# First attention of a four-layer Flamingo-style block: layer norms, counts and positions on GpSimd, the queries' high part on ScalarE

## The chip, the cores and the metric

The kernel runs on one core of a Trainium2 chip. The metric is the device time of one execution in microseconds. The core has TensorE (PE), VectorE (DVE), ScalarE (ACT), GpSimd (POOL) and SyncE (SP, which here only starts transfers). Each engine works through its own list of instructions in order and waits on semaphores that others raise.

## What is computed

`x` is (4, 1024, 256), float32; the context has 4 x 154 rows.

```
x = x + tanh(g_xattn[0]) * attention0(layernorm(x), ctx)      # stablemax weights: s >= 0: s + 1, else 1 / (1 - s)
x = x + tanh(g_ffn[0])   * moe(layernorm(x))                  # 64 experts, top 8, at most 128 tokens each, plus a shared part
x = x + tanh(g_xattn[1]) * attention1(layernorm(x), ctx)      # softmax
x = x + tanh(g_ffn[1])   * butterfly_mlp(layernorm(x))
```

A token that goes to expert e gets the place "how many tokens before it chose e"; from place 128 on it is dropped. The places feed the lists of tokens by expert.

## The kernel before

The 4096 tokens lie in SBUF as 32 tiles of 128 x 256. They are worked on in 8 halves of 512 tokens (4 tiles). There are three stages with a barrier of all engines between them: the first attention with the routing (0 to 401 us), the experts with the shared part (401 to about 740 us), the second attention with the last layer. The change lies in the first stage.

A plan (`plan_first`) is a list of units such as `("norm", "q", h)` or `("count", h)`. Every engine runs through the same list and executes its own part of each unit, so that the order on all engines follows the list. Attention scores come in chunks: 20 a half, 160 in all. For each chunk PE makes the scores (L811, or L813 and L814), ACT squares and takes the reciprocal root (L1174, L1179), DVE makes the weight with a minimum and a maximum (`weight`, L1505), which also frees the bank of the scores, and PE multiplies with the values (L839, L834). The scores have five banks, so PE can't make chunk n before DVE has made weight n - 4 or so.

Between the chunks the plan puts the steps of the neighbouring halves, one step at a time:

- `query_steps`: statistics (`stats`, DVE, L1380 and L1389), reciprocal deviation (`rstd`, POOL, L1889 and L1894), the norm of four tiles into `normed` (`norm`, DVE, L1425), transposes (PE, L757), `q_feats` (ACT, L1143), the projection (PE, L800, two parts), `q_parts` (DVE: L1496 adds the bias and rounds to the high part, L1499 makes what is left), and transfers into the query stack (`send_q`, SP).
- `after_steps`: transposes back and division (L856, L1511, L1513), the output projection (L880, L885), `x_add` (DVE, L1526), statistics and norm into `rows` (same lines as above), transposes (L757), `send_rows`, gate logits (L900), `shift`, `top`, `pick` (DVE, L1535 to L1558: the mask of the eight chosen experts), `count` (PE: the counts of the tokens before, by products with masks and with the running sum `before`; DVE: four additions of a mask to that sum, L1582), `position` (DVE: L1591 to L1605) and, in halves 3 and 7, `gate_weights`.
- `keys_steps` for the next batch entry, beside halves 0, 2 and 4: `key_mask`, `key_rest`, `set_values` on DVE among others.

The statistics of a norm have two sets of buffers (`moments`, `rstd`), taken in turn. POOL has little else in this stage: it clears tiles at the start and makes `rstd` 16 times. After the last scores, one-hot tiles (`hots`, DVE, L1710 and L1713; ACT, L1273) are made from the positions and PE places them (L998), 18 of 32 tiles within the first stage.

```
            def weight(n):
                V.wait_ge(exped, n + 1)
                V.scalar_tensor_tensor(weights[n % 9][:, :], weights[n % 9][:, :], 1.0, score_bank[n % 5], ALU.min,
                                       ALU.max).then_inc(weighted, 1)
```

Of the kernel before, what the change touches and what calls it, by code (L numbers as in the profile page):

```python
# [18 lines left out]
P = 128  # L19
# [37 lines left out]
NB = 16  # L57
# [3 lines left out]
FAR = 4096.0  # L61
ZERO_ROWS = (TILES + 1) // 3
# [422 lines left out]
def build(nc, D, out):  # L485
    ctx = ExitStack()
    with ctx:
# [50 lines left out]
        with ExitStack() as scope:  # L538
# [48 lines left out]
            pos_i = s0("pos_i", [P, 2, HT, EXPERTS], I32)  # L587
# [57 lines left out]
        with ExitStack() as scope:  # L645
# [43 lines left out]
        pool_set, ln_var, ln_rstd, x_added, out_biased, hid_split = (  # L689
            sem(n) for n in ("pool_set", "ln_var", "ln_rstd", "x_added", "out_biased", "hid_split"))  # L690
# [3 lines left out]
        keys_split, queries_split, weighted, masked, rows_set, summed = (  # L694
            sem(n) for n in ("keys_split", "queries_split", "weighted", "masked", "rows_set", "summed"))
# [444 lines left out]
        def scalar_program(A):  # L1140
# [219 lines left out]
            units = {"key_round": key_round, "send_keys": send_keys, "lay_wk": lay_wk, "q_feats": q_feats_, "square": square,  # L1360
# [15 lines left out]
        def vector_program(V):  # L1376
# [27 lines left out]
            def norm(kind, h):  # L1404
                n = norm_no[kind, h]
                if kind == "q":
                    to = normed
                    if h:
                        V.wait_ge(*misc.filled(("turn_q", h - 1), CD - 1))
                elif kind == "r":  # L1410
                    to = rows
                    if h:
                        V.wait_ge(*misc.filled(("turn_rows", h - 1), CD - 1))
                        V.wait_ge(rows_out, 16 * h)
                else:
                    to = normed1
                    if kind == "f":
                        last_turn = ("turn_q1", h + 2) if h + 2 < HALVES else ("turn_f", h - 1)
                    else:
                        last_turn = ("turn_f", h - 3) if h >= 3 else ("turn_q1", h - 1)  # L1420
                    if (kind, h) != ("q1", 0):
                        V.wait_ge(*wide.filled(last_turn, CD - 1))
                V.wait_ge(ln_rstd, n + 1)
                for t in range(HT):
                    V.tensor_scalar(to[:, t, 0:DIM], x[:, HT * h + t, :], moments[n % 2][:, t, 0:1],  # L1425
# [65 lines left out]
            def q_parts(h, mo):  # L1491
                key = ("project_q", h, mo)
                if h and mo == 0:
                    wait_all(V, q_in[(h - 1) % 2], (h - 1) // 2 + 1)
                V.wait_ge(*misc.filled(key))
                V.tensor_scalar(q_stage[:, 0, mo, :], misc.ap(key), bq[:, mo:mo + 1], None,  # L1496
                                ALU.add).then_inc(queries_rounded, 1)
# [53 lines left out]
            def pick(h):  # L1551
# [5 lines left out]
                V.wait_ge(dve_own, own.n)  # L1557
                V.tensor_scalar(masks[:, :, :], picked[:, :, :], 0.0, None, ALU.is_gt).then_inc(masked, 1)  # L1558
# [15 lines left out]
            def count(h):  # L1574
                old, new = before[:, h % 2, :], before[:, (h + 1) % 2, :]
                V.wait_ge(masked, h + 1)
                for t in range(HT):
                    if t:
                        V.wait_ge(dve_own, own.n)
                    elif h:  # L1580
                        V.wait_ge(summed, h)
                    m = V.tensor_tensor(new, new if t else old, masks[:, t, :], ALU.add)  # L1582
                    if t < HT - 1:
# [740 lines left out]
```

## Time and profile before

| | us |
|---|---|
| Median of 3 runs | 1207.16 (1202.42 to 1209.33) |
| The profiled execution, its own time | 1211.06 |
| Its span, first to last instruction | 1209.2 |

| engine | busy us in the whole span | share |
|---|---|---|
| PE | 1030.5 | 85% |
| DVE | 790.1 | 65% |
| ACT | 624.0 | 52% |
| POOL | 384.1 | 32% |

Busy time is time with an instruction in execution; a group's row gives its sum, the mean of one in ns, and after the second bar the idle time of the engine just before it with what ended that. A timeline row has start, duration, engine, line and instruction, and in brackets the idle time before it. The chain of waits is the work that ended last, followed back from the end: where a piece stands on it, nothing shown would have let what follows start earlier.

### The profile page before, as it was taken

Reading aid. Unit: us, or ns where it says so; the run is one execution under the profiler, and the core shown is the slowest. Engines: PE = TensorE matmul, PEld = TensorE weight load, DVE = VectorE, ACT = ScalarE, POOL = GpSimd, SP = SyncE. Lnnn points to the kernel's source line nnn. Section 1 sums busy time; section 2 is a strip of 40 time slices with the busy share of each in tenths; the row PEclk is TensorE's granted clock in tenths of the full one; section 3 lists DMA queues with packets and bytes.
Section 4 is the critical chain, followed back from the end, with each engine's and each line's share of the span. In section 5 each row is a group of like instructions: output and inputs, shape, how many; then the busy total and the mean of one; then the engine's idle time right before and its main releaser. Section 6 shows DMA issues by size and latency. Waiting matters only on the chain.

```text
span 1209.2 us, 17329 instructions
## 1 busy us (share of the span) xinstructions
PE 1030.5 (85%) x5635; PEld 750.4 (62%) x5635; DVE 790.1 (65%) x1991; ACT 624.0 (52%) x1185; POOL 384.1 (32%) x385
## 2 busy tenths in 40 slices
PE   3998898698876679989898967889888988999987
PEld 2445455354444567878687757567676766767666
DVE  5677877866777756664667566766757575664433
ACT  2786656757846425564554431455545554544532
POOL 6000000000000023776767622233434243514234
PEclk9798979979997889999999995899999999999989
DMA  6564542632121434888878653421322232120001
GB/s 156 147 160 131 156 133 69 184 108 53 49 105 53 143 116 91 187 215 232 200 190 181 127 140 72 113 83 29 104 54 75 68 88 71 51 56 1 20 1 35
DMA packets 101561, 128.41 MB, mean 106 GB/s; under 512 B 31136, under 2 KB 73504, under 8 KB 101216
## 3 DMA queue, kind: packets, MB, share of 16 engines
q1 hardware_dynamic: 87088, 106.32, 30.8%
q0 software_dynamic: 12288, 18.88, 8.7%
q10 hardware_dynamic: 2096, 2.10, 0.8%
q8 instruction: 46, 0.75, 0.3%
q14 instruction: 43, 0.35, 0.1%
HBM read 66.15 MB, written 30.70 MB: 80 GB/s over the span
## 4 chain that ended last, share of the span: by engine, by line
PE 55%; DVE 25%; ACT 6%; issue 5%; POOL 3%; DMA 2%; ACTq 1%; SPq 0%; DVEq 0%; POOLq 0%
PE psum L1118 6%; PE psum L932 6%; PE psum L1103 5%; PE psum L839 4%; PE psum L1021 4%; PE psum L811 4%; PE psum L948 4%; DVE stats L1380 3%; PE psum L885 3%; DVE weights L1505 2%; DVE peaks L1790 2%; PE psum L834 2%; PE psum L800 2%; PE psum L1050 2%; PE psum L757 2%
## 5 line engine op out<-in xcount | busy, mean ns | idle before, releaser
L1889 POOL TENSOR_SCALAR vareps<-moments 128x4 f32<-128x4 f32 x32 | 10.4, 324 | 483.8 <-DVE moments L1389 483.8
L811 PE MATMUL psum<-q_stack,k_stack 97*128 97x512 f32 (+1 forms) x256 | 124.1, 513 | 38.6 <-DVE weights L1505 21.4
L1316 ACT ACTIVATE weights<-psum 128x512 f32<-128x512 f32 x160 | 93.8, 595 | 69.5 <-PE psum L811 59.5
L1909 POOL DMA_INDIRECT expert_sums<-made,sum_rows x64 | 104.9, 1639 | 62.5 <-DVE made L1754 43.0
L1505 DVE SCALAR_TENSOR_TENSOR weights<-weights,psum 128x512 f32<-128x512 f32 x160 | 101.8, 679 | 22.5 <-ACT weights L1179 22.3
L1790 DVE TENSOR_REDUCE peaks<-psum 128x2 f32<-128x308 f32 x256 | 107.0, 470 | 12.3 <-PE psum L1052 12.0
L1050 PE MATMUL psum<-k_stack,q_stack 96*128 96x256 f32 x256 | 86.4, 391 | 28.6 <-DVE peaks L1790 16.7
L932 PE MATMUL psum<-feat_parts,w_shared_up 128*128 128x512 f32 x384 | 98.3, 406 | 6.4 <-DVE shared_silu L1628 2.8
L1174 ACT ACTIVATE weights<-psum 128x512 f32<-128x512 f32 x160 | 88.8, 594 | 28.9 <-PE psum L811 28.5
L1118 PE MATMUL psum<-w_con_high,hidden 128*128 128x256 f32 x512 | 103.3, 300 | 0.5 <-POOL hidden L1941 0.5
L1941 POOL TENSOR_TENSOR hidden<-hidden_whole,hidden 128x512 fp32r<-128x512 f32 x64 | 82.4, 1293 | 63.8 <-DVE hidden L1838 63.8
L1901 POOL DMA_INDIRECT got<-rows_scratch,tokens x64 | 68.4, 1069 | 99.8 <-DVE sum_rows L1741 80.6
L811 PEld LDWEIGHTS psum<-q_stack,k_stack 97*128 97x128 f32 (+1 forms) x256 | 50.0, 200 | 79.3 <-issue 44.6
L1838 DVE CAST hidden<-hidden_whole 128x512 fp32r<-128x512 f32 x64 | 44.8, 704 | 81.2 <-ACT hidden_whole L1345 80.6
L1179 ACT ACTIVATE weights<-weights 128x512 f32<-128x512 f32 x160 | 94.0, 634 | 1.0
L1103 PE MATMUL psum<-feats,w_up_high 128*128 128x512 f32 x256 | 79.7, 408 | 14.2 <-ACT hidden_whole L1345 8.9
L1118 PEld LDWEIGHTS psum<-w_con_high,hidden 128*128 128x128 f32 x512 | 81.6, 192 | 14.0 <-POOL hidden L1941 6.9
L1050 PEld LDWEIGHTS psum<-k_stack,q_stack 96*128 96x128 f32 x256 | 52.9, 207 | 53.4 <-DVE peaks L1790 21.9
L932 PEld LDWEIGHTS psum<-feat_parts,w_shared_up 128*128 128x128 f32 x384 | 71.7, 193 | 22.0 <-DVE shared_silu L1628 3.6
L1021 PEld LDWEIGHTS psum<-got_t,expert_w 128*128 128x128 f32 x512 | 65.8, 195 | 24.9 <-ACT got_t L1280 15.9
L1021 PE MATMUL psum<-got_t,expert_w 128*128 128x128 f32 x512 | 72.1, 285 | 10.5 <-DVE inner L1747 5.5
L839 PE MATMUL psum<-weights,values 128*32 128x512 f32 x512 | 78.0, 675 | 0.7 <-ACT turned L1186 0.7
(212 smaller groups left out, 2315.7 us busy)
## 6 DMA issues: line engine op xcount, KB each, us to landing
expert_w<-in_expert_w SPq DMA_DIRECT2D x64, 384.0 KB
q_stack<-q_stage SPq DMA_DIRECT2D x96, 128.0 KB, 2.5
q_stack<-q_stage SPq DMA_DIRECT2D x174, 64.0 KB, 2.0
expert_sums<-zeros SPq DMA_DIRECT2D x6, 1408.0 KB, 8.1
fetched<-expert_sums SPq DMA_DIRECT2D x14, 512.0 KB, 4.9
k_raw<-in_k SPq DMA_DIRECT2D x16, 300.0 KB
x<-in_x SPq DMA_DIRECT2D x8, 512.0 KB, 4.5
rows_scratch<-rows SPq DMA_DIRECT2D x8, 512.0 KB, 2.9
```

What stands on the lines that cost most here:

```text
L811: T.matmul(to, k[0:row, head_at(head), :], q[0:row, head // 2, :], start=True, stop=True).then_inc(scored, 1)
L839: m = T.matmul(to[32 * j:32 * j + 32, :], vals[:, 0, 4 * g + j, :], w[(n + j) % len(w)][:, :], start=True, stop=False, tile_position=(0, 3 ...
L932: m = T.matmul(shared_banks(h).ap(key, half), w_sgu[:, pw, a:a + P], sh_parts[:, pf, c * HALF:(c + 1) * HALF], start=n == 0 and c == 0, st ...
L1021: m = T.matmul(bank[2][:, part * P:(part + 1) * P], expert_w[e % 8][:, c, part * INNER:(part + 1) * INNER], got_t[e % 3][:, c, :], start=c ...
L1050: T.matmul(view[:, :, 0:P], q[0:STACK, p, t * P:(t + 1) * P], keys[0:STACK, 2 * p:2 * p + 2, :], start=True, stop=True)
L1103: m = T.matmul(wide.ap(key), up_parts[pw][:, c, k * P:(k + 1) * P], feats[:, pf, c, :], start=i == 0 and c == 0, stop=i == 2 and c == CD - 1)
L1118: m = T.matmul(out_bank[t // 2][:, t % 2 * DIM:(t % 2 + 1) * DIM], hidden[k][:, ph, t * P:(t + 1) * P], con_parts[pw][:, BURST * b + k, :] ...
L1179: A.activation(weights[n % 9][:, :], weights[n % 9][:, :], ACT.Abs_reciprocal_sqrt).then_inc(exped, 1)
L1316: A.activation(weights1[n % 6][:, :], score_bank[n % 2], ACT.Exp).then_inc(exped, 1)
L1505: V.scalar_tensor_tensor(weights[n % 9][:, :], weights[n % 9][:, :], 1.0, score_bank[n % 5], ALU.min, ALU.max).then_inc(weighted, 1)
L1790: V.tensor_reduce(peaks[h % 2][:, t, 2 * p:2 * p + 2], view, AX.X, ALU.max).then_inc(wide.frees(key, i), 1)
L1909: G.indirect_dma_start(sum_dram[e % SUMS], bass.IndirectOffsetOnAxis(ap=sum_rows[:, e:e + 1], axis=0), made[e % 4][:, :], None, bounds_che ...
```

## The change

The layer norms of kind "q" (queries) and "r" (rows) are written by POOL, right behind its `rstd`, and no longer by DVE; DVE keeps the norms of the second attention and the last layer. The high part of the queries is made by ACT (Identity with the bias) instead of DVE. The running sum of masks (`count`) is made by POOL and left out for the last half, where nobody reads it. Of `position` DVE keeps the instruction that reads PSUM; six instructions on POOL, in float32 instead of integers, follow. Waits are added where an engine now reads what another writes: DVE's aggregate of moments waits for the norm that read that buffer (two norms back), `pick` for `summed`, `position` and `hots` for `positioned`.

```
-                V.tensor_scalar(q_stage[:, 0, mo, :], misc.ap(key), bq[:, mo:mo + 1], None,
-                                ALU.add).then_inc(queries_rounded, 1)
+            def q_parts(h, mo):                                    # ScalarE
+                key = ("project_q", h, mo)
+                if mo == 0:
+                    if h:
+                        wait_all(A, q_in[(h - 1) % 2], (h - 1) // 2 + 1)
+                    else:
+                        A.wait_ge(wq_in, 32)
+                A.wait_ge(*misc.filled(key))
+                A.activation(q_stage[:, 0, mo, :], misc.ap(key), ACT.Identity,
+                             bias=bq[:, mo:mo + 1]).then_inc(queries_rounded, 1)
...
+                if kind in ("q", "r") and n >= 2:                  # VectorE, statistics
+                    V.wait_ge(ln_normed, HT * (n - 1))
...
-            def count(h):                                          # VectorE
-                old, new = before[:, h % 2, :], before[:, (h + 1) % 2, :]
...
-                V.scalar_tensor_tensor(picked[:, :, :], masks[:, :, :], -FAR, counts, ALU.mult,
+                if h:
+                    V.wait_ge(positioned, h)
+                V.scalar_tensor_tensor(ranks[:, 0, :, :], masks[:, :, :], -FAR, counts, ALU.mult,
                                        ALU.add).then_inc(misc.frees(key), 1)
-                V.wait_ge(*misc.freed(key))
-                V.tensor_scalar(picked[:, :, :], picked[:, :, :], FAR, None, ALU.add)...
-                V.tensor_copy(pos_i[:, 0, :, :], picked[:, :, :])...
-                V.tensor_scalar(pos_i[:, 1, :, :], pos_i[:, 0, :, :], 4, None, ALU.logical_shift_right)...
-                V.tensor_scalar(pos_i[:, 0, :, :], pos_i[:, 0, :, :], NB - 1, None, ALU.bitwise_and)...
-                V.tensor_copy(pos_a[:, HT * h:HT * h + HT, :], pos_i[:, 1, :, :])
-                V.tensor_copy(pos_b[:, HT * h:HT * h + HT, :], pos_i[:, 0, :, :])
...
+            def norm_first(n, h, to, turned_before):               # GpSimd, called at the end of rstd
+                if h:
+                    G.wait_ge(*misc.filled(turned_before, CD - 1))
+                G.wait_ge(ln_rstd, n + 1)
+                for t in range(HT):
+                    G.tensor_scalar(to[:, t, :], x[:, HT * h + t, :], moments[n % 2][:, t, 0:1],
+                                    rstd[n % 2][:, t:t + 1], ALU.subtract, ALU.mult).then_inc(ln_normed, 1)
...
+            def count(h):                                          # GpSimd
+                if h == HALVES - 1:
+                    return
+                ...                                                # waits for masks, for PE's last count, four additions
+            def position(h):                                       # GpSimd, each waits for the one before
+                G.wait_ge(*misc.freed(("count", h)))
+                block, first = rank_block[:, :, :], ranks[:, 0, :, :]
+                G.tensor_scalar(block, first, BLOCK_MIDDLE, 1.0 / NB, ALU.subtract, ALU.mult)...
+                G.tensor_scalar(block, block, WHOLE, 0.0, ALU.add, ALU.add)...
+                G.tensor_scalar(block, block, -WHOLE, 0.0, ALU.add, ALU.add)...
+                G.tensor_scalar(pos_a[:, HT * h:HT * h + HT, :], block, FAR / NB, 0.0, ALU.add, ALU.add)
+                G.tensor_scalar(ranks[:, 1, :, :], block, float(-NB), 0.0, ALU.mult, ALU.add)...
+                G.tensor_tensor(pos_b[:, HT * h:HT * h + HT, :], ranks[:, 1, :, :], first, ALU.add).then_inc(positioned, 1)
```

## Rows read from the trace of the kernel before

**Rows 1.** Windows of the span: busy us (count) by engine, clock, DMA share, GB/s.
```profile
30.00:346.00 316.00, 275.01 (x1239) 151.89 (x1239) 236.21 (x651) 211.72 (x399) 16.43 (x26) 0.90 0.43 118
346.00:401.00 55.00, 30.93 (x180) 23.25 (x180) 41.27 (x105) 28.37 (x40) 1.56 (x2) 0.84 0.20 71
```

**Rows 2.** Waits of PE from 60 to 340 us: total, times, longest.
```profile
PE psum L811 <- DVE weights L1505: 19.9, 16, 3.4
PE psum L757 <- DVE rows L1425: 5.0, 7, 1.4
PE psum L757 <- DVE probs L1540: 3.5, 3, 1.5
```

**Rows 3.** Timeline of PE around the count and position of half 2.
```profile
191.91 1.00 PE L811 MATMUL psum<-q_stack,k_stack 97*128 97x512 f32 x2 [1.26 <-DVE weights L1505]
...
195.28 1.22 PE L811 MATMUL psum<-q_stack,k_stack 97*128 97x512 f32 x2 [1.49 <-DVE weights L1505]
```

**Rows 4.** Chain of waits, 186 to 196 us: start, us, piece.
```profile
190.31 0.19 DVE mask_sums L1582
...
191.17 1.20 DVE weights L1505 x2
192.36 0.34 DVE picked L1591
...
192.73 0.30 DVE picked L1594
...
194.53 0.61 DVE weights L1505
```

**Rows 5.** Chain of waits, 208 to 224 us, beside the keys' steps.
```profile
213.07 1.29 DVE rows L1425 x4
...
217.62 1.04 POOL rstd L1894
...
218.76 1.39 DVE normed L1425 x4
...
222.61 0.40 DVE probs L1540
```

**Rows 6.** Groups of DVE to 480 us: busy us, mean ns, idle before.
```profile
L1496 DVE TENSOR_SCALAR q_stage<-psum,bq 128x512 fp32r<-128x512 f32 x16 | 12.0, 748 | 18.3 <-PE psum L800 18.2
L1425 DVE TENSOR_SCALAR normed<-x,moments,rstd 128x256 f32<-128x256 f32 x32 | 11.0, 409 | 6.7 <-POOL rstd L1894 6.7
```

**Rows 7.** Groups of POOL, in both parts of the span (split at 480 us).
```profile
L1894 POOL TENSOR_TENSOR rstd<-vareps,minus_half 128x4 f32<-128x4 f32 x16 | 16.7, 1044 | 2.2
...
L1959 POOL MEMSET zeros<- 128x256 f32 x1 | 0.3, 316 | 0.1
...
L1928 POOL TENSOR_TENSOR x<-x,fetched 128x256 f32<-128x256 f32 x56 | 40.1, 746 | 49.2 <-DMA fetched<-expert_sums 39.6 <-DVE k_stack L1774 8.5 <-POOL x L1928 0.2
...
L1941 POOL TENSOR_TENSOR hidden<-hidden_whole,hidden 128x512 fp32r<-128x512 f32 x64 | 82.4, 1293 | 63.8 <-DVE hidden L1838 63.8
```

**Rows 8.** Groups of ACT to 480 us.
```profile
L1143 ACT ACTIVATE q_feats<-psum 128x512 f32<-128x512 f32 x16 | 9.2, 597 | 27.6 <-PE psum L757 27.6
...
L1228 ACT ACT_TABLE_LOAD x2 | 2.6, 1283 | 0.0
```

**Rows 9.** Timeline, the end of the stage: the last rows' norm.
```profile
362.65 1.25 POOL L1894 TENSOR_TENSOR rstd<-vareps,minus_half 128x4 f32<-128x4 f32 x1
...
369.69 1.38 DVE L1425 TENSOR_SCALAR rows<-x,moments,rstd 128x256 f32<-128x256 f32 x4
370.25 2.00 PE L757 MATMUL psum<-ident,rows 128*128 128x128 f32 x7 [8.86 <-DVE rows L1425]
```

**Rows 10.** Chain of waits, the last transfer before the barrier.
```profile
397.07 3.82 DMA rows_scratch<-probs
```

**Rows 11.** Timeline of the start.
```profile
8.14 1.38 DVE L1425 TENSOR_SCALAR normed<-x,moments,rstd 128x256 f32<-128x256 f32 x4 [1.57 <-POOL rstd L1894]
...
18.81 0.84 ACT L1156 ACTIVATE k_stage<-k_masked 128x768 fp32r<-128x768 f32 x1 [6.47 <-DVE k_masked L1465]
```

More of the change, by code:

```diff
@@ L61 @@
 FAR = 4096.0
+BLOCK_MIDDLE, WHOLE = (NB - 1) / 2, 1.5 * 2 ** 23
 ZERO_ROWS = (TILES + 1) // 3
@@ L1572, in gate_weights @@
                                        ALU.mult, ALU.mult).then_inc(rows_set, 1)
-            def count(h):
-                old, new = before[:, h % 2, :], before[:, (h + 1) % 2, :]
[L1576 to L1583, printed above, removed]
-                        m.then_inc(dve_own, own.up())
-                m.then_inc(summed, 1)
             def position(h):
@@ L1709, in hots @@
                     V.wait_ge(placed, i - HOTS + 1)
+                V.wait_ge(positioned, i // HT + 1)
                 V.tensor_tensor(hot_a[i % HOTS][:, :, :, :], a_iota[:, :, :, :],
@@ L1873, in gpsimd_program @@
         def gpsimd_program(G):
-            set_ = Own()
+            set_, own = Own(), Own()
             def clear_values(vals):
@@ L1894, in norm_rstd @@
                 G.tensor_tensor(rstd[n % 2][:, :], vareps[n % 2][:, :], half_pow[:, :], ALU.pow).then_inc(ln_rstd, 1)
+                if kind == "q":
+                    norm_first(n, h, normed, ("turn_q", h - 1))
+                elif kind == "r":
+                    if h:
+                        G.wait_ge(rows_out, 16 * h)
+                    norm_first(n, h, rows, ("turn_rows", h - 1))
+            def norm_first(n, h, to, turned_before):
+                if h:
+                    G.wait_ge(*misc.filled(turned_before, CD - 1))
[3 more added lines that the diff above has]
+                                    rstd[n % 2][:, t:t + 1], ALU.subtract, ALU.mult).then_inc(ln_normed, 1)
             def gather(e):
@@ L1942, in hidden_rest @@
                                 ALU.subtract).then_inc(hid_split, 1)
+            def count(h):
+                if h == HALVES - 1:
+                    return
+                old, new = before[:, h % 2, :], before[:, (h + 1) % 2, :]
+                G.wait_ge(masked, h + 1)
+                if h:
+                    G.wait_ge(*misc.filled(("count", h - 1)))
+                if h:
+                    G.wait_ge(summed, h)
+                for t in range(HT):
+                    if t:
+                        G.wait_ge(pool_own, own.n)
+                    m = G.tensor_tensor(new, new if t else old, masks[:, t, :], ALU.add)
+                    if t < HT - 1:
+                        m.then_inc(pool_own, own.up())
+                m.then_inc(summed, 1)
+            def position(h):
+                G.wait_ge(*misc.freed(("count", h)))
+                block, first = rank_block[:, :, :], ranks[:, 0, :, :]
+                G.tensor_scalar(block, first, BLOCK_MIDDLE, 1.0 / NB, ALU.subtract, ALU.mult).then_inc(pool_own, own.up())
+                G.wait_ge(pool_own, own.n)
+                G.tensor_scalar(block, block, WHOLE, 0.0, ALU.add, ALU.add).then_inc(pool_own, own.up())
+                G.wait_ge(pool_own, own.n)
+                G.tensor_scalar(block, block, -WHOLE, 0.0, ALU.add, ALU.add).then_inc(pool_own, own.up())
+                G.wait_ge(pool_own, own.n)
+                G.tensor_scalar(pos_a[:, HT * h:HT * h + HT, :], block, FAR / NB, 0.0, ALU.add, ALU.add)
+                G.tensor_scalar(ranks[:, 1, :, :], block, float(-NB), 0.0, ALU.mult, ALU.add).then_inc(pool_own, own.up())
+                G.wait_ge(pool_own, own.n)
+                G.tensor_tensor(pos_b[:, HT * h:HT * h + HT, :], ranks[:, 1, :, :], first, ALU.add).then_inc(positioned, 1)
             def set_query_ones(i):
@@ L1972, in gpsimd_program @@
             G.wait_ge(pool_set, set_.n)
-            units = {"rstd": norm_rstd, "load_rest": clear_rest, "gather": gather, "down": scatter,
+            units = {"rstd": norm_rstd, "count": count, "position": position, "load_rest": clear_rest, "gather": gather, "down": scatter,
                      "add_experts": add_experts, "bias_out": bias_out, "up": hidden_rest, "clear_v1": clear_v1}
```

53 lines of the change are left out of this document (16 added, 37 removed).

## The prediction

> **What bounds the kernel now.** I read the busy shares by window first, then PE's waits, then the chain of waits and the timeline at the places that they point to. From 30 to 346 us PE is busy 275 of 316 us, DVE 236, ACT 212 and POOL only 16 [rows 1]. PE is the bound, but 41 us of this stretch it stands still. The waits say for what: half of its idle time from 60 to 340 us is the wait for a weight of DVE [rows 2], and the timeline shows two pauses of one size, 1.26 and 1.49 us, at every half [rows 3]; I found the pair at halves 0, 1, 2, 3 and 4 (in half 3 the second is 3.4 us, the longest of rows 2, since `gate_weights` joins it) and the same chain of DVE pieces at half 5. The chain shows what DVE did instead of weights: the four additions of `count` before the first pause, the seven instructions of `position` before the second [rows 4]. So the stage isn't bound by DVE's sum, it is bound by DVE's bursts. From 346 to 401 us DVE is the bound itself, busy 41 of 55 us [rows 1], and what ends the stage is the transfer of `probs`, which starts when DVE is through with position and gate weights [rows 10]. Nothing behind the barrier is touched.
>
> **What leaves DVE.** 64 norm tiles at 0.41 us (the row has half of them), 16 high parts at 0.75 [rows 6], 32 additions at 0.19, and six instructions of `position` eight times, 0.30 each [rows 4]. That is 26 + 12 + 6 + 14 = 58 us, some 54 if the overlap of neighbours is taken out (four norm tiles take 1.38 us together [rows 9]). This isn't the gain: only what PE or the stage's end waited for counts. Step by step:
>
> **Count and position, halves 0 to 5.** Without `count` (190.31 to 191.17) the two weights start 0.86 us earlier, and a little more since DVE no longer makes the high part: ACT does it in about 0.60 in place of 0.76. I take 1.0 of the 1.26. Of `position` DVE keeps the 0.34 us piece; the 1.8 us from 192.73 to 194.53 go [rows 4]. The root that the next weight needs is done long before, so the second pause closes in full: 1.5. 6 x 2.5 = **-15.0 us**. POOL's part of position is six dependent instructions. By the bounds below some 0.6 us each, 3.6 us; only `hots` of half 7's tiles, which come behind the barrier, could meet it late, and POOL is idle there. I cost it at nothing; should it be 3 us late it would still end before the transfer of rows 10 lands. POOL's load in a half is then about 2.7 (rstd and variance, twice) + 4.4 (eight norm tiles) + 1.4 (count) + 3.6, 12 of 43 us: not a bound.
>
> **The price of a norm tile on POOL.** No row shows this instruction there. The lower bound is a clear of the same 128x256 tile, 0.32 us, which reads nothing; the upper one is an addition of two such tiles, 0.75 [rows 7]. It reads one tile, so it lies between; I take the middle, 0.55. Four tiles: 2.2 us against 1.38 on DVE.
>
> **Norm of the rows (8 times).** It lies on PE's path: `x_add`, statistics, rstd, norm, transposes. The tiles come one by one and PE transposes behind them; before, the first is ready 0.42 us after the start, now 0.55, and the last 2.2 instead of 1.38. In the four halves without keys' steps (1, 3, 5 and 6) the transposes end about 0.8 us later, but DVE, which normed there after a wait for rstd, has its next weights 1.4 us earlier and more. I take a net **+0.5 each, +2.0 us**. In halves 0, 2 and 4 DVE is the chain [rows 5]: rows 1.29, later a wait for POOL's rstd (1.04) and normed 1.39, then the keys' rest, weights and probs, for which PE waits 3.5 us in three times [rows 2]. These three pieces go off DVE, 3.7 us; POOL's rows end at about the same time as DVE's did, since they start at once and not behind the keys' masks. PE's pauses there are up to 1.4 us for rows and 1.5 for probs [rows 2]. Of these 2.9 I take **-2.0 each, -6.0 us**: behind DVE, PE's own gate products come due next. The norm of the queries is covered by the chunks' work between it and its transposes: PE's waits of rows 2 are for rows and never for normed. If that cover were gone it would cost 0.8 us a half, as with rows.
>
> **The queries' high part.** 16 activations of 128x512 from PSUM, 0.60 each [rows 8], in place of 0.75 on DVE. DVE waited 18.3 us in all for the projection before them [rows 6]; ACT, which is in order too, now waits there, and squares and roots queue behind it. DVE still waits, for ACT. ACT is idle around the second part in every half (its busy sum is 212 of 316 us), so I cost it at **0**; bounds: +9.6 us if every activation delays a root that is due, -2.4 if the shorter time shows every time.
>
> **The end of the stage.** The last norm of rows was ready for DVE at 363.9 but began at 369.69, behind DVE's splitting of the shared weights; PE waited 8.9 us for it [rows 9]. POOL does it at once. But the next consumer, ACT's row features, stands behind one-hot tiles that DVE makes, and DVE works on without a break: so only DVE's own 1.38 us come off, **-1.4**. Half 6: count and position, 2.8 us of DVE, lie between the last weight and the divisions for which PE and ACT wait: **-2.8**. Half 7: the same, right ahead of the gate weights and the last transfer [rows 10]: **-2.8**. Sum **-7.0 us**.
>
> **The start.** Before the first scores everything is one chain. The first norm on POOL ends 0.8 us later than DVE's 1.38 [rows 11], the high parts save 0.15 to 0.3, and ACT's second high part now comes before its rounding of the keys (0.84), which eats that. **+0.6 us.** POOL's clearing starts 0.8 later; DVE's first values wait for it, but its first weights wait for ACT's root behind that, which covers it.
>
> **Sum.** -15.0 + 2.0 - 6.0 + 0 - 7.0 + 0.6 = -25.4 us. The profiled execution took 1211.06 us, so its like would take 1185.7. It stands 3.9 us above the median of the runs, 1207.16; from the median I get 1181.8, and forecast **1182**.
>
> **A rule against it.** The rstd that ran while DVE compared one-hot tiles took 1.25 us [rows 9], the mean is 1.04 [rows 7]; most of the others ran beside nothing but weights. So POOL is slowed by some DVE work. The Trainium skill, "SBUF — State Buffer", on the shared port pair, says why: a DVE instruction with two SBUF inputs and a GpSimd instruction that reads SBUF exclude each other for its whole length; the trace agrees with a delay of that kind. DVE's weights read one input from PSUM and are no such instruction by that rule; the one-hot comparisons are.
>
> **Rivals.**
> (a) *DVE and POOL exclude each other at the end of the stage.* There DVE makes one-hot tiles all the time, and POOL gets 2.2 us of norm and twice 3.6 of position, plus a count of 1.4: 10.8 us. If DVE stood still for as long as POOL runs, the 7.0 gained are gone and 3.8 more: 1182 + 10.8 = 1193. For: the 1.25 us. Against: what was slowed there is POOL, and only by 0.2.
> (b) *ACT takes the place of DVE.* Each half's two high parts (9.6 us in all) delay roots, and ACT takes over DVE's wait for the projection, up to 12.4 of the 18.3 us in the steady stretch. All of it would leave -25.4 + 22 = -3.4: 1204. For: the roots follow the squares at once in ACT's list. Against: ACT's idle time.
> (c) *Slower: the norm on POOL is dear.* Rows' norms are on the path eight times with four tiles each, so each 0.1 us on a tile is 3.2 us. The gain is gone at 0.55 + 25.4 / 32 = 1.34 us a tile; at 1.5 the time is 1212. Nearest row for: 128x512 with two inputs takes 1.29 [rows 7], and a mere 4 elements with `pow` 1.04. Against: that is twice the tile and twice the inputs.
> (d) *Slower: ACT reloads its table.* If Identity isn't in the set that holds the root, each high part brings two loads of 1.28 us [rows 8]: 16 x 2.56 = 41 us on ACT, time 1223. Against: ACT's copies of this stage need none.
> (e) *More is gained.* PE's clock is 0.90 on average there [rows 1] because it falls to 1.2 GHz for stretches; with fewer pauses it may fall less. With all pauses of rows 2 closed and some of that, -40: 1167.
>
> **How the numbers follow.** The forecast's case gets 0.66, its own range 1171 to 1195 (half to all of the pauses, a tile from 0.32 to 0.75, which alone is -7 to +6 us); (a) 0.12, (b) 0.08, (c) 0.04, (d) 0.02, (e) 0.08. A measurement of this kernel can tell about 0.5% (6 us) from no change. Faster by more than that: 0.66 + 0.12 + 0.08 = 0.86; within: (b), 0.08; slower: 0.06. The range that leaves out 2 in 10 is 1168 to 1198: it holds (a), and leaves out most of (e), (b), (c) and (d).
>
> **What the profile would show.** Right: the pauses of PE before L811 in each half fall from 1.26 and 1.49 to under 0.3 and 0; norm tiles on POOL take 0.4 to 0.75 us; rows' transposes begin as soon as their norm does, and no pause there is over 1.5; the barrier falls near 376 us in place of 401; DVE's busy time falls by some 54 us, ACT's rises by 9.6; the other stages keep their lengths within 2 us. Wrong: tiles above 1 us on POOL, table loads between chunks, PE waiting for ACT's roots after the projection (b), one-hot comparisons longer than before (a), or the same pauses with a new releaser.

## The result and the profile after

| | before | after |
|---|---|---|
| Median | 1206.72 (1202.12 to 1211.06, 11 runs) | 1220.64 (1213.09 to 1223.28, 11 runs) |
| Ratio after / before | | 1.0115, 95% interval 1.0094 to 1.0136 |
| Profiled execution, its span | 1211.06, 1209.2 | 1222.56, 1220.8 |
| Barrier behind the first attention (PE's first product of the next stage) | 401.04 | 413.02 |
| From the barrier to the end | 808.2 | 807.8 |
| Busy: PE, DVE, ACT, POOL | 1030.5, 790.1, 624.0, 384.1 | 1036.8, 741.9, 633.0, 519.7 |

The kernel became slower by 1.15% (some 14 us), where 25 us were to be gained. The loss lies in the first stage alone: its barrier comes 12.0 us later, and what follows takes as long as before (807.8 against 808.2). DVE did lose its work (-48 us busy) and ACT took the 9 us that were forecast. Both profiled executions are slower than their medians, by 4.3 and 1.9 us. So the question is what in the first stage ate 37 us, from the forecast barrier at 376 to the measured 413.

Here are the busy shares of the kernel after by window, for the same two stretches as [rows 1] (busy us and count of PE, PE's weight loads, DVE, ACT, POOL; granted clock; DMA share; GB/s):

```profile
30.00:346.00 316.00, 268.32 (x1194) 148.07 (x1194) 188.44 (x496) 218.77 (x412) 126.97 (x144) 0.87 0.44 120
346.00:401.00 55.00, 36.04 (x188) 24.49 (x188) 36.68 (x97) 25.64 (x38) 17.83 (x16) 0.80 0.19 67
```

In the same 316 us PE issued 45 matmuls fewer than in [rows 1], at a granted clock of 0.87 in place of 0.90. POOL went from 16 to 127 us, and DVE is idle for 128 us. PE's waits from 60 to 340 us, which answer to [rows 2] (total, times, longest):

```profile
PE psum L760 <- POOL rows L1888: 24.2, 26, 1.4
PE psum L814 <- DVE weights L1507: 7.4, 11, 1.8
PE psum L760 <- POOL normed L1888: 3.4, 4, 0.9
```

The waits for DVE's weights fell from 19.9 to 7.4 us, as the steps on count and position wanted. But the wait of the transposes for rows rose from 5.0 us in 7 times to 24.2 in 26: PE now waits for each tile by itself. The groups of POOL show why (busy us, mean ns; these answer to [rows 7]):

```profile
L1888 POOL TENSOR_SCALAR rows<-x,moments,rstd 128x256 f32<-128x256 f32 x32 | 42.9, 1352 | 1.6 <-POOL rstd L1875 1.5
L1888 POOL TENSOR_SCALAR normed<-x,moments,rstd 128x256 f32<-128x256 f32 x32 | 38.7, 1221 | 1.3 <-POOL rstd L1875 1.2
L1959 POOL TENSOR_SCALAR rank_block<-ranks 128x256 f32<-128x256 f32 x8 | 8.7, 1089 | 48.1 <-DVE ranks L1584 48.0
...
L1966 POOL TENSOR_SCALAR ranks<-rank_block 128x256 f32<-128x256 f32 x8 | 3.5, 444 | 0.5
```

A norm tile takes 1.22 us on POOL, not 0.55, and lies outside the bound of 0.75 that an addition of two such tiles gave. (The 1.35 in the rows' line is a mean that the last four tiles raise; see the end of the stage.) The prediction had named tiles above 1 us as a sign that it was wrong. L1959 (subtract, multiply) and L1966 (multiply, add) read and write tiles of the same form, 128x256 of f32, with constants as factors, and differ in the pair of operations: 1.09 against 0.44 us. The high part on ACT took 0.69 us a piece (0.60 forecast), with no table load beside it:

```profile
L1192 ACT ACTIVATE q_stage<-psum,bq 128x512 fp32r<-128x512 f32 x16 | 11.0, 686 | 19.5 <-PE psum L803 19.5
```

A second thing shows when the stage is cut at the statistics of the rows of halves 5, 6 and 7. Two windows, first of the kernel before, then of the kernel after, with the same 145 and 139 matmuls in them:

```profile
298.92:329.75 30.83, 27.33 (x145) 15.22 (x144) 24.35 (x70) 25.04 (x48) 1.26 (x2) 1.00 0.14 48
329.75:362.19 32.44, 24.45 (x139) 14.22 (x138) 25.92 (x78) 15.65 (x27) 1.26 (x2) 1.00 0.26 98
```

```profile
297.68:335.03 37.35, 32.29 (x145) 18.30 (x144) 20.92 (x56) 25.11 (x48) 12.76 (x17) 0.82 0.12 40
335.03:374.56 39.53, 28.99 (x139) 16.66 (x138) 23.35 (x64) 15.76 (x27) 13.34 (x17) 0.83 0.22 80
```

Up to here the kernel after was 1.2 us ahead (297.68 against 298.92). It loses 13.6 us in these two. Of this 9.5 us is PE's busy time (27.33 to 32.29, 24.45 to 28.99) for the same products: the granted clock fell from 1.00 to 0.82. The timeline of PE shows the place:

```profile
298.22 1.09 PE L814 MATMUL psum<-q_stack,k_stack 97*128 97x512 f32 x2
300.68 0.30 PE L760 MATMUL psum<-ident,rows 128*128 128x128 f32 x1 [1.37 <-POOL rows L1888]
301.79 0.33 PE L760 MATMUL psum<-ident,rows 128*128 128x128 f32 x1 [0.82 <-POOL rows L1888]
302.99 0.33 PE L760 MATMUL psum<-ident,rows 128*128 128x128 f32 x1 [0.87 <-POOL rows L1888]
304.19 1.33 PE L760 MATMUL psum<-ident,rows 128*128 128x128 f32 x5 [0.87 <-POOL rows L1888]
...
309.19 3.51 PE L903 MATMUL psum<-gate_w,row_feats 128*128 128x65 f32 x16
```

```profile
298.00:304.00 6.00, 2.02 (x6) 0.79 (x5) 2.57 (x5) 2.69 (x5) 5.73 (x5) 0.98 0.02 4
304.00:306.00 2.00, 1.81 (x7) 1.46 (x7) 0.00 (x0) 1.04 (x2) 0.14 (x1) 0.50 0.47 157
306.00:316.00 10.00, 10.00 (x33) 6.04 (x32) 4.51 (x18) 4.62 (x10) 0.00 (x0) 0.50 0.33 113
```

PE is busy for 2.0 of 6 us in the waits for four tiles; behind them the clock stands at 0.50 (1.2 GHz) for 12 us, and the gate logits take 3.51 us, 1.90 in undisturbed halves. The waits cost a second time here, after they are over.

The end of the stage, the last rows' norm (answers to [rows 9]):

```profile
376.48 9.03 POOL L1888 TENSOR_SCALAR rows<-x,moments,rstd 128x256 f32<-128x256 f32 x4 [0.21 <-POOL rstd L1875]
377.51 2.36 DVE L1592 TENSOR_TENSOR w_shared_up<-shared_staging,w_shared_up 128x1024 fp32r<-128x1024 f32 x2 [1.19 <-ACT w_shared_up L1226]
377.85 0.45 PE L760 MATMUL psum<-ident,rows 128*128 128x128 f32 x1 [4.09 <-POOL rows L1888]
379.79 1.22 DVE L1597 TENSOR_TENSOR feat_parts<-feats_m,feat_parts 128x1024 fp32r<-128x1024 f32 x1
380.92 1.42 DVE L1601 TENSOR_TENSOR w_shared_down<-shared_staging,w_shared_down 128x1024 fp32r<-128x1024 f32 x1
381.99 0.48 PE L760 MATMUL psum<-ident,rows 128*128 128x128 f32 x1 [3.69 <-POOL rows L1888]
```

Four tiles take 4.84 us elsewhere and 9.03 here. PE had the first tile at 377.85, the second at 381.99, the third at 384.26. So the second took some 4.2 us: it lay beside DVE's four splits with two SBUF inputs (377.51 to 382.34) and was ready only 0.35 us before the last of them ended. The third took 2.3 us, beside DVE's one-hot comparisons. DVE hardly suffered (one split 1.42, the others of their kind 1.22). At the start (answers to [rows 11]) nothing covers the first norm; the first scores come at 30.89, where they came at 27.16 before:

```profile
8.33 4.84 POOL L1888 TENSOR_SCALAR normed<-x,moments,rstd 128x256 f32<-128x256 f32 x4
...
30.89 1.19 PE L814 MATMUL psum<-q_stack,k_stack 97*128 97x512 f32 x2 [5.97 <-DMA k_stack<-k_stage]
```

### The profile page after: what moved, and what is told of

Its sections match the earlier page's. It is cut to its first block, busy times and chain, and to the rows that moved or that the text cites. A ratio compares the mean times of both kernels' runs of the same rounds, so it can differ in the third digit from the quotient of the medians.

```text
span 1220.8 us, 17380 instructions
## 1 busy us (share of the span) xinstructions
PE 1036.8 (85%) x5635; PEld 755.4 (62%) x5635; DVE 741.9 (61%) x1831; ACT 633.0 (52%) x1201; POOL 519.7 (43%) x525
## 4 chain that ended last, share of the span: by engine, by line
PE 55%; DVE 17%; POOL 10%; ACT 8%; issue 6%; DMA 2%; SPq 1%; ACTq 1%; DVEq 0%; POOLq 0%
PE psum L935 5%; PE psum L1121 5%; PE psum L842 4%; PE psum L1106 4%; PE psum L1024 4%; PE psum L814 4%; PE psum L951 4%; POOL rows L1888 3%; PE psum L888 3%; PE psum L837 3%; PE psum L760 2%; PE psum L1053 2%; DVE stats L1394 2%; DVE peaks L1771 2%; PE psum L803 2%
## 5 line engine op out<-in xcount | busy, mean ns | idle before, releaser
L1177 ACT ACTIVATE weights<-psum 128x512 f32<-128x512 f32 x160 | 88.2, 594 | 20.6 <-PE psum L814 20.6
```

## The experiments

A ratio stands against runs of the kernel before on the same chip in the same job, with its 95% interval; 0.001 of it is 1.2 us. "Barrier" is PE's first product of the next stage in the profiled execution (before 401.04, after 413.02). That is one execution of each kernel, and two pairs of them show how far it can be trusted: with the high part alone changed the barrier came 5.2 us sooner (395.82) at a ratio of 1.0012, and with quicker positions in the multiply-add kernel it came 6.0 us later (389.25 against 383.22) at an unchanged ratio. Differences of some 6 us between barriers tell nothing by themselves; the length of a piece of the stage that an edit touches is steadier.

**Which part costs, which gains.** Both norms (queries and rows) back on DVE, all the rest of the change kept:

```
+on_vector = lambda kind, h: kind in ("q", "r")
...
-                if kind in ("q", "r"):                             # VectorE's norm
+                if kind in ("q", "r") and not on_vector(kind, h):
                     return
```

> The changed kernel with both first-stage norms back on VectorE; count, position and the queries' high part stay moved. Theory A (the price of a norm tile on GpSimd, 1.22 us where I took 0.55, is the whole of the loss; the rest gains what I forecast): about -20 us against the kernel before, so 1185 to 1190, the pauses before the scores gone, the first scores at 27 us again. Rival B (the moved count, position or high part cost something as well, for instance by ScalarE's roots coming later): 1200 or more.

Measured 1183.88 us, ratio 0.9769 (0.9715 to 0.9823), barrier 375.65; it is a little below the expected 1185 to 1190. Counts, positions and high part together gain 28 us, and the norms on POOL lose 42 on top of them (0.0346). The complement, norms alone on POOL (counts, positions and high part back on DVE):

> The kernel before with only the norms of queries and rows on GpSimd. Theory A: the loss of the changed kernel (+14) and the gain of the other parts (-20) come apart: 1235 to 1245, with both pauses per half (1.26 and 1.49 us) still there. Rival B: near the changed kernel, 1215 to 1222.

Measured 1240.94, ratio 1.0253 (1.0199 to 1.0307), barrier 434.28: slower by 31 us. PE waits 22.4 us for rows there from 60 to 340 us, and the 18.2 us for weights are back. The same norms cost 31 us here and 42 where the other parts had moved: the two losses seem to hide a part of each other. The difference of 11 us (0.0093) is only just clear of the noise of these runs (0.008).

The first of these divided again. The high part alone on ACT (`q_parts` as in the change, everything else as before):

> The kernel before with one part of the change: ScalarE makes the queries' high part; norms, counts and positions stay on VectorE. The prediction costed this at 0 (bounds +9.6 and -2.4), and gave count and position all of the -25 us that remain with the norms on VectorE. If that is right: 1206 to 1211 us and the same pauses before PE's chunk scores as in the kernel before. Rival: ScalarE's high parts lengthen the chain of roots (rival b): 1212 to 1218. Other rival: the high part brings a gain of its own, since VectorE's weights no longer queue behind its 0.75 us, twice a half: 1195 to 1204.

Measured 1207.78, ratio 1.0012 (0.9992 to 1.0031): no difference. PE's pauses for weights stay:

```profile
PE psum L814 <- DVE weights L1517: 20.2, 17, 2.6
```

Counts and positions alone on POOL:

> The kernel before with another part alone: counts and positions on GpSimd, high part and norms on VectorE. By the prediction's terms (-15.0 in halves 0 to 5, -5.6 at the end of the stage) about 1188 us, 1184 to 1192, and the pair of pauses of PE at count and position (1.26 and 1.49 us) gone but for some tenths. Rival: the high part is worth half of the gain of 25 us that both have together, then 1195 to 1200.

Measured 1187.00, ratio 0.9829 (0.9791 to 0.9866), barrier 377.94, and the pauses are down to

```profile
PE psum L815 <- DVE weights L1523: 5.6, 10, 0.8
```

That is -20.6 us by the ratio; the forecast's two terms were -15.0 and -5.6. The high part on top of it may give some us (0.9769 against 0.9829, intervals that overlap; barrier 2.3 us earlier); this isn't settled.

**Which of the norms.** The whole change, with rows on DVE and queries on POOL:

> The changed kernel with the norm of the rows back on VectorE, that of the queries still on GpSimd. Theory A: what is left of the loss is the start (first scores at 31 us, +3.7) and nothing in the loop, since the queries' norm is covered: 1188 to 1196. Rival (the queries' norm costs as much as the rows'): 1204 or more.

Measured 1208.85, ratio 0.9989 (0.9951 to 1.0028), barrier 396.75: in the range of the rival, not of the theory. The queries' norm is not covered. With it alone on POOL the transposes wait for single tiles:

```profile
PE psum L761 <- POOL normed L1901: 10.8, 13, 0.9
```

The projection behind them runs at a lower clock (granted 0.57 from 183.5 to 187.0 us):

```profile
180.77 0.33 PE L761 MATMUL psum<-ident,normed 128*128 128x128 f32 x1 [0.88 <-POOL normed L1901]
181.97 0.77 PE L761 MATMUL psum<-ident,normed 128*128 128x128 f32 x5 [0.88 <-POOL normed L1901]
...
183.54 3.38 PE L804 MATMUL psum<-q_feats,wq 128*128 128x512 f32 x4 [0.33 <-ACT q_feats L1147]
```

With both norms on DVE the same projection ran at a granted clock of 1.00 (169.5 to 172.0 us):

```profile
169.51 1.98 PE L804 MATMUL psum<-q_feats,wq 128*128 128x512 f32 x4 [0.22 <-ACT q_feats L1147]
```

The fourth corner, queries on DVE and rows on POOL:

> The whole change, but the queries' norm stays on VectorE and the rows' norm is on GpSimd with tiles of 1.2 us. The fourth corner of a square: both norms on VectorE 1183.9, both on GpSimd 1220.6, queries' alone on GpSimd 1208.9. If the two norms cost independently, 1220.6 - 25 = 1196 us (1192 to 1200), with no pause of PE at the start of the span and rows waits of some 24 us in the steady stretch. If they share one queue and block each other, the rows' norm alone costs more than 12 us and the time is 1200 to 1210.

Measured 1214.54, ratio 1.0067 (1.0030 to 1.0104), barrier 405.53: outside both ranges. Against both on DVE, rows alone cost 36 us (0.0298), queries alone 27 (0.0220), both 42 (0.0346). Each alone costs much, and they overlap, although each has its own tiles and its own time on POOL. A plain delay on the path would add up.

**Does the clock add to what the waits cost?** The whole change, and PE fills the waits between tiles with work that has no use:

```
                         m = T.transpose(ring.ap(key, c)[:, t * P:(t + 1) * P], src[:, t, c * P:(c + 1) * P],
                                         ident[:, :])
+                        if c == 0 and t < HT - 1 and kind[0] in ("q", "r"):
+                            for _ in range(4):
+                                T.transpose(ring.ap(key, c)[:, t * P:(t + 1) * P], src[:, t, c * P:(c + 1) * P],
+                                            ident[:, :])
```

> The whole change, and PE repeats the transpose of a tile four times (some 0.2 us each) while it waits for the next tile of a norm that GpSimd makes; data, order and all other engines are untouched, and PE only gets more work. Theory: the waits of 0.9 us for single tiles cost twice, once as idle time and once because the granted clock falls to 1.2 GHz behind them (in halves 6 and 7 PE's same work took 32.3 and 29.0 us in place of 27.3 and 24.5). Then the clock stays up: 1205 to 1213 us, granted clock of the first 401 us at 0.90 or more. Rival: only the waiting itself costs, and the clock falls for another reason; then the time is 1220 or some us more.

Measured 1207.82, ratio 0.9988 (0.9960 to 1.0017), barrier 399.78. PE got 192 matmuls more and the kernel became some 13 to 15 us faster than the whole change. In half 6, behind the rows' transposes, and then the window of 316 us:

```profile
296.60 1.08 PE L818 MATMUL psum<-q_stack,k_stack 97*128 97x512 f32 x2
...
299.17 1.90 PE L907 MATMUL psum<-gate_w,row_feats 128*128 128x65 f32 x16
```

```profile
30.00:346.00 316.00, 275.78 (x1419) 161.28 (x1418) 197.07 (x527) 222.25 (x418) 133.84 (x154) 0.95 0.45 124
```

The tiles come no sooner, but the gate logits behind them take 1.90 us and not 3.51, and the mean clock is 0.95 and not 0.87. Nothing else was changed, so the 13 to 15 us are the clock's. Not all of them belong to the 42 us that the norms cost. Two come at the start (first scores at 28.92 in place of 30.89), where PE's first projection took 3.75 us in the changed kernel and 1.96 with the filling; but it had taken 3.61 in the kernel before. First before, then with the filling:

```profile
11.65 3.61 PE L800 MATMUL psum<-q_feats,wq 128*128 128x512 f32 x4 [0.73 <-ACT q_feats L1143]
```

```profile
15.09 1.96 PE L807 MATMUL psum<-q_feats,wq 128*128 128x512 f32 x4 [0.73 <-ACT q_feats L1150]
```

And the mean clock of 0.95 is above the 0.93 of the kernel with both norms on DVE. How much of the 42 us the clock makes isn't split further.

**The price of a tile.** The same norm on POOL as multiply, then add, with two small instructions for the shift:

```
+                G.tensor_tensor(by[:, :], moments[n % 2][:, :, 0], rstd[n % 2][:, :], ALU.mult)...
+                G.tensor_scalar(by[:, :], by[:, :], -1.0, 0.0, ALU.mult, ALU.add)...
...
-                    G.tensor_scalar(to[:, t, :], x[:, HT * h + t, :], moments[n % 2][:, t, 0:1],
-                                    rstd[n % 2][:, t:t + 1], ALU.subtract, ALU.mult)...
+                    G.tensor_scalar(to[:, t, :], x[:, HT * h + t, :], rstd[n % 2][:, t:t + 1],
+                                    by[:, t:t + 1], ALU.mult, ALU.add)...
```

> The changed kernel with the norm on GpSimd written as multiply, then add (x * rstd + shift, two small instructions for the shift) instead of subtract, then multiply. In the changed kernel's profile a GpSimd TENSOR_SCALAR of the same tile takes 0.40 us as multiply-add and 1.07 to 1.10 as add-add or subtract-multiply. Theory C (the order of operations sets the price): a tile takes 0.4 to 0.5 us, four 1.8, and the time falls to 1185 to 1195. Rival (the factors that are read per partition set it, not the operations): a tile stays at 1.2 us and the time at 1221 or a little above.

Measured 1194.14, ratio 0.9879 (0.9828 to 0.9929), barrier 383.22. The tile has nearly the price that the prediction took:

```profile
L1894 POOL TENSOR_SCALAR rows<-x,rstd,shift_by 128x256 f32<-128x256 f32 x32 | 23.0, 729 | 0.8
...
L1894 POOL TENSOR_SCALAR normed<-x,rstd,shift_by 128x256 f32<-128x256 f32 x32 | 17.4, 555 | 0.8
```

So the pair of operations alone is worth some 28 us (1.0115 to 0.9879). The rows' mean of 729 hides the last four tiles:

```profile
346.56 7.73 POOL L1894 TENSOR_SCALAR rows<-x,rstd,shift_by 128x256 f32<-128x256 f32 x4
```

They take 7.73 us beside DVE's splits and comparisons, where four take 2.18 elsewhere. The quicker instruction helps little there (7.73 against 9.03): PE had the second tile at 350.86 and the third at 353.13, 3.6 and 2.3 us after the one before, where it had been 4.1 and 2.3 with the slow tile.

Which pairs are quick, tried on the position's instructions (norms on DVE; written so that the positions stay the same):

```
-    G.tensor_scalar(block, first, BLOCK_MIDDLE, 1.0 / NB, ALU.subtract, ALU.mult)...
-    G.tensor_scalar(block, block, WHOLE, 0.0, ALU.add, ALU.add)...
-    G.tensor_scalar(block, block, -WHOLE, 0.0, ALU.add, ALU.add)...
-    G.tensor_scalar(pos_a[...], block, FAR / NB, 0.0, ALU.add, ALU.add)
+    G.tensor_scalar(block, first, -BLOCK_MIDDLE, 1.0 / NB, ALU.add, ALU.mult)...
+    G.tensor_scalar(block, block, 1.0, -WHOLE, ALU.mult, ALU.subtract)...
+    G.tensor_scalar(block, block, WHOLE, None, ALU.subtract)...
+    G.tensor_scalar(pos_a[...], block, 1.0, FAR / NB, ALU.mult, ALU.add)
```

> Norms on VectorE, and the operations of a position on GpSimd written with other pairs that give the same numbers: (add, multiply), (multiply, subtract), subtract alone, (multiply, add). A measurement of the instruction's price by its pair, 128x256 each. Theory A, a multiply in first place is the quick form: 1.07, 0.40, 1.07 and 0.40 us. Theory B, only (multiply, add) is quick: 1.07, 1.07, 1.07, 0.40. Theory C, any instruction with one multiply and one add is quick, whatever the order, and subtract is slow: 0.40, 1.07, 1.07, 0.40. The time of the whole kernel isn't the question: 1180 to 1187.

The four groups, in the order of the plus lines L1972, L1974, L1976, L1978:

```profile
L1974 POOL TENSOR_SCALAR rank_block<-rank_block 128x256 f32<-128x256 f32 x8 | 9.0, 1129 | 0.7
L1976 POOL TENSOR_SCALAR rank_block<-rank_block 128x256 f32<-128x256 f32 x8 | 8.2, 1020 | 0.7
...
L1978 POOL TENSOR_SCALAR w_con_fused<-rank_block 128x256 bf16<-128x256 f32 x8 | 3.4, 430 | 0.7
L1972 POOL TENSOR_SCALAR rank_block<-ranks 128x256 f32<-128x256 f32 x8 | 3.4, 426 | 53.9 <-DVE ranks L1595 53.8
```

(add, multiply) 0.43, (multiply, subtract) 1.13, subtract alone 1.02, (multiply, add) 0.43: theory C. (One run, 1183.57 us.) These means hold single long ones; the medians of the eight are 0.41, 1.09, 0.86 and 0.41. One multiply and one add is quick in either order; subtract is slow, in a pair or alone, and so is (add, add), 1.07 to 1.10 by the medians of the changed kernel.

Positions quick as well, in the whole change and with the norms on DVE:

> The whole change in the same places, with GpSimd's operations in the order multiply, then add: x * rstd + shift for the norms (1194 us alone) and the same for the four slow operations of a position. Theory: on GpSimd this pair takes 0.40 us for 128x256 where (subtract, multiply) and (add, add) take 1.07; each position then takes about 2.9 us in place of 5.6. Positions were covered, so the time stays at 1190 to 1196. Rival: the positions of the last halves hold up the one-hot tiles; then 1186 to 1190.

> Norms on VectorE; high part on ScalarE; counts and positions on GpSimd, positions as multiply, then add. Without that last point 1183.9. If GpSimd's positions are covered: 1181 to 1186. Rival: some of their 5.6 us is on the path at the stage's end, then 1176 to 1181.

Measured, first the whole change: 1193.71, ratio 0.9879 (0.9829 to 0.9928), where quick norms alone gave 0.9879 as well. Then with the norms on DVE: 1183.44, ratio 0.9810 (0.9730 to 0.9889), where slow positions gave 0.9769. No change can be measured in either, so nothing shows that POOL's 5.6 us for a position hold anything up.

**The two ends.** The whole change, with only the last rows' norm (`(kind, h) == ("r", HALVES - 1)`) on DVE, and with only the very first norm (`("q", 0)`) there:

> The whole change, but the norm of the last half's rows is made by VectorE. On GpSimd these four tiles took 9.03 us beside VectorE's splitting of the shared weights and PE stood still 9.6 us for them in three times, in place of 8.9 us in one. If exclusion of the two engines at the stage's end (rival a) is what the last norm costs, the time falls by 3 to 7 us: 1214 to 1218. If the end is bound by VectorE's own work, it doesn't fall: 1219 to 1223, as VectorE gets 1.4 us more of work.

> The whole change, but the very first norm (queries of half 0, before any score) is made by VectorE. The first scores came 3.7 us later with it on GpSimd, where nothing covers it. Theory: these 3.7 us come off in full: 1215 to 1218. Rival: the keys' transfer or PE's clock, whose low stretches move with the start, take part of it or add to it: outside 1213 to 1219.

Measured 1216.48, ratio 1.0077 (1.0046 to 1.0108), and 1216.34, ratio 1.0078 (1.0043 to 1.0113). Each is worth some 4.5 us (0.0038, 0.0037) by the middle values, but the intervals overlap with that of the whole change, and the traces are sharper. With the first norm on DVE the scores come at 27.20, 3.69 us sooner, and the barrier 3.6 sooner (409.39). For the last rows' norm take the time from the last `vareps` (behind the last statistics, ahead of the norm) to the barrier. First the kernel after, then the one with this norm on DVE:

```profile
374.56 0.32 POOL L1870 TENSOR_SCALAR vareps<-moments 128x4 f32<-128x4 f32 x1 [15.06 <-DVE moments L1405]
```

```profile
369.93 0.32 POOL L1881 TENSOR_SCALAR vareps<-moments 128x4 f32<-128x4 f32 x1 [15.10 <-DVE moments L1406]
```

Their barriers are at 413.02 and 406.33, so the piece takes 38.46 and 36.40 us: the last norm on POOL costs 2.1. It is 36.40 as well with both norms on DVE, and 38.47 with the rows alone on POOL. The other 4.6 us of the earlier barrier lie ahead of the edit and aren't its work.

**What is left at the price that was forecast.** Multiply, then add, and one repeated transpose to fill the 0.24 us that PE now waits for a tile:

> Norms on GpSimd as multiply, then add (a tile 0.55 us, the price that the prediction assumed; 1194 us instead of the 1182 forecast), and PE repeats the transpose of a tile once while it waits 0.24 us for the next. If the missing 12 us are the clock, which fell to 0.81 and 0.88 in two halves there: the clock of the halves rises to 0.95 or more and the time is 1182 to 1189. If they are the plain sequence on the path (rstd, two small instructions, the first tile, and the start, 2.7 us later): 1191 to 1196.

Measured 1182.13, ratio 0.9792 (0.9756 to 0.9827), barrier 380.17. That is the forecast time, but the filling isn't shown to be worth the 12 us. The two profiled executions are 7.7 us apart (spans 1188.0 and 1180.3), and the barrier moved by 3.0 of them (383.22 to 380.17). The other 4.7 us lie behind it, in stages that this edit doesn't touch and that took 800.1 us here and 803.7 to 810.5 in all the other profiled executions.

All mended at once: as the last one, and besides the first norm and the last rows' norm on DVE, positions quick:

> The kernel with norms as multiply, then add, and PE's one repeated transpose (1182.1 us), and besides the very first norm and the last rows' norm back on VectorE and positions as multiply, then add. If the start's 2.4 us (first scores at 29.3 or so in place of 26.9) and the exclusion at the stage's end (the last norm took 7.7 us there in place of 2.2) are plain delays on the path: 1174 to 1179. If they are hidden or eaten by the clock's low stretches: 1180 to 1184.

Measured 1184.16, ratio 0.9812 (0.9784 to 0.9840), barrier 376.22. The barrier is 3.95 us sooner, but the two ends make only 1.5 of it: the first scores come at 27.43 in place of 28.38 (0.95, where 2.4 had been expected), and from the last `vareps` to the barrier it is 36.59 in place of 37.18. The other 2.4 us lie between, where only the quicker positions were changed, which gained nothing before. Behind the barrier it took 806.3 us and not 800.1. The total shows no gain and lies just above the range of the rival. So all versions from 1182 to 1184 are equal within what these runs tell: the simplest of them, norms left on DVE, beats the kernel before by 2.3% (1.8 to 2.9).

## Why the prediction was wrong, step by step

- **Count and position, halves 0 to 5, and halves 6 and 7 at the end** (-15.0 and -5.6): held. Alone they gave -20.6 us (the interval is 4.5 us to either side), PE's wait for weights fell from 19.9 to 5.6 us, and from the last `vareps` to the barrier the time fell from 38.85 us in the kernel before to 36.40, where the step had 2.8 for half 7. The mechanism was right: DVE's bursts, not its sum.
- **The queries' high part** (0): held, alone 1.0012; whether it gains some us on top of the moved counts stays open (0.9769 against 0.9829). A piece took 0.69 us, not 0.60. Rivals (b) and (d) didn't happen: no loss shows, and no table was loaded beside it.
- **The price of a norm tile on POOL**: this step failed. It was bounded by 0.32 and 0.75, "an addition of two such tiles", as if a form with fewer inputs could not cost more. It measured 1.22. No row before showed a (subtract, multiply) on POOL, and the upper bound came from another operation; the `pow` on 4 elements, 1.04 us, warned that POOL's price depends on the operation. By the prediction's own 3.2 us per 0.1, the 0.67 us too little make 21; with the tile at its price (multiply, then add) the kernel is 28 us faster, and still 12 above the forecast (1194.14 against 1182). Rival (c) put break-even at 1.34 us a tile and the time at 1.5 at 1212; what came was 1220.64 at 1.22. The rival had the right cause and sign and too low a price: it counted rows only, and no clock.
- **"The norm of the queries is covered by the chunks' work"**: failed. PE waited for `normed` nowhere in [rows 2] because DVE made four tiles in 1.38 us. With 4.84 us the cover was gone: alone on POOL they cost 27 us (3.7 of them at the start), where the step's "if that cover were gone" had 0.8 us a half.
- **Norm of the rows** (+2.0, and -6.0 in the keys' halves) and the norm's part in **the end of the stage** (-1.4): with the tile at 0.55 and the waits filled, the kernel stands at 0.9792, with the norms on DVE at 0.9769. By the middle values that is 3 us more and not 4.8 less, as the norm's terms and the start's together promised; the intervals are too wide to exclude either. So at the assumed price, too, no gain from taking the norms off DVE is shown. That this kernel's 1182.13 us is the forecast time is luck: the other parts gained 28 us (0.9769), where 20.6 were forecast for them.
- **The clock**: it stood in the prediction only as a gain, in rival (e). It is the term that was missing. Behind waits tile by tile the granted clock fell, to 0.50 for 12 us in half 6, and filling the waits gave 13 to 15 us back, a part of them at a place (the start) where the clock had cost as much before the change.
- **The end of the stage, rival (a)**: something like the exclusion happened, but to POOL. DVE went on and POOL's four tiles took 9.03 us in place of 4.84; undone, the end was 2.1 us shorter. The Trainium skill, "SBUF — State Buffer", "SBUF: two separate sides", says that whoever comes first holds the shared ports for its whole instruction and the other blocks. The trace agrees in so far as a tile of 1.22 us took 4.2 beside the splits of 1.22, and one split took 1.42. Which engine held the ports when, no trace shows.
- **The start** (+0.6): 3.7 us, by the tile's price again (4.84 against 1.38 us is 3.46).

At the barrier, forecast for 376 and measured at 413.0, the pair of operations makes some 30 us (413.02 to 383.22, with its share of the clock; 24 by the other kernel with quick norms, at 389.25). The rest, some 7 us, went with the filling and the two ends together (to 376.22), but single steps of 3 and 4 us in it can't be told from what barriers move by themselves.

What stays open: why the costs of the two norms overlap (27 and 36, together 42). PE's waits from 60 to 340 us show a part of it: it waits 10.8 us for the queries' norm when that alone is on POOL, but only 3.4 when the rows' norm is there too. The mean clock of 30 to 346 us is 0.93 with both on DVE, 0.91 with queries, 0.88 with rows and 0.87 with both on POOL, so the second doesn't take the clock down as far as the first; that fits as well, but neither was tested by itself.

## What to carry to other kernels

Before work goes to GpSimd, look for a row with that very pair of operations there, and try it with one multiply and one add; an instruction with another operation gives no bound. Where TensorE waits tile by tile for a slower producer, it can cost twice, as here: once in waiting and once in the clock behind it. Check the granted clock in windows around such waits. A change that takes work off an engine gains only what somebody waited for: the counts and positions, 20 us of DVE's work, gave 20.6, and the norms, 26 us of it, no gain that shows. "Covered" holds only for the duration that was seen: say how long the cover is.

## What the runs showed that was not expected

- GpSimd's two-operation instruction on 128x256 of f32 takes 0.40 to 0.41 us as (multiply, add) or (add, multiply) with constants and 0.55 with values by partition, but 1.07 to 1.22 as (subtract, multiply), (multiply, subtract) or (add, add), and 0.86 as subtract alone (medians). The Trainium skill, "GPSIMD Engine Reference", "Engine selection", calls one-input work on GpSimd roughly line-rate against DVE; the quick pair comes near to that (0.55 against DVE's 0.41 in [rows 6]), the slow one doesn't (1.22).
- Useless transposes made the kernel faster: 192 more of them, and 1220.6 became 1207.8 us.
- Four waits of PE of 0.8 to 1.4 us, none of them long, stood ahead of 12 us at a granted clock of 0.50. With the last three mostly filled, the gate logits behind them took 1.90 us and not 3.51.
